# State-space stage of a four-layer forward pass: two of four tiles' sums by accumulating transfers, the dt projection in two halves, and one decay factor computed earlier on ScalarE

## The reference, cut to what matters

```python
xm, z = split(x @ W_in.T)                       # 512 channels each
xc = silu(causal_conv4(xm) + conv_b)
dt, Bm, Cm = split(xc @ W_xproj.T, [64, 64 + 16])
delta = softplus(dt @ W_dt.T + b_dt)
A = -exp(A_log)                                 # 512 x 16
h_t[:, n] = exp(delta_t * A[:, n]) * h_{t-1}[:, n] + delta_t * Bm_t[n] * xc_t     # n = 0..15
y_t = sum over n of Cm_t[n] * h_t[:, n] + D_skip * xc_t
out = (y * silu(z)) @ W_out.T
```

## Time and profile before

| | us |
|---|---|
| median of 3 runs | 2458.88 (2457.44 to 2459.68) |
| the profiled execution | 2460.9 |
| its span | 2459.2 |
| busy: PE / DVE / ACT / POOL over the span | 1911.8 / 1678.1 / 1184.7 / 1515.8 |
| the 8 halves of the loop, about | 68 to 1131 |

### The profile page before, as it was taken

How to read it: one execution, slowest core, us unless ns; L and a number is a source line. 1 busy time by engine, 2 the same in 40 slices (tenths; PEclk the granted TensorE clock), 3 DMA queues, 4 the chain that set the end, 5 groups by cost and what they waited for, 6 DMA issues and landing times. The chain is left out here.

```text
span 2459.2 us, 35798 instructions
## 1 busy us (share of the span) xinstructions
PE 1911.8 (78%) x10252; PEld 1465.2 (60%) x10253; DVE 1678.1 (68%) x3193; ACT 1184.7 (48%) x2021; POOL 1515.8 (62%) x1152
## 2 busy tenths in 40 slices
PE   6787879686979787875599999907877784799970
PEld 2445455554555454544499999904655664699970
DVE  1779898989989898985644444437634897644438
ACT  2677777777777767773232222226632441111112
POOL 1799999999999999994133333335622420355532
PEclk9888979798989888887699999958988896799995
DMA  3111111111101011112411111142000014122226
GB/s 123 38 35 40 39 37 36 39 39 37 39 23 52 27 49 31 43 36 77 165 48 47 47 48 48 41 139 77 9 18 11 9 35 163 42 71 70 70 65 192
DMA packets 76780, 138.63 MB, mean 56 GB/s; under 512 B 10369, under 2 KB 47873, under 8 KB 75858
## 3 DMA queue, kind: packets, MB, share of 16 engines
q1 hardware_dynamic: 62994, 99.67, 12.4%
q0 software_dynamic: 13632, 37.24, 4.8%
HBM read 104.86 MB, written 32.01 MB: 56 GB/s over the span
## 5 line engine op out<-in xcount | busy, mean ns | idle before, releaser
L787 DVE TENSOR_TENSOR_SCAN a_hs<-a_dA,a_carry,a_hs 128x512 f32<-128x512 f32 x512 | 628.3, 1264 | 63.5 <-ACT a_dA L559 53.7
L399 POOL TENSOR_TENSOR a_hs<-a_u,a_b_bc 128x1024 f32<-128x1024 f32 (+1 forms) x292 | 634.9, 2182 | 2.3 <-POOL a_u L381 1.9
L929 PE MATMUL a_h_ps<-k_ident,a_hs 128*128 128x128 f32 x2064 | 328.3, 308 | 174.7 <-DVE a_acc L750 95.6
L929 PEld LDWEIGHTS a_h_ps<-k_ident,a_hs 128*128 128x128 f32 x2064 | 268.4, 158 | 293.5 <-DVE a_hs L787 86.2
L559 ACT ACTIVATE a_dA<-a_delta,a_a_neg 128x512 f32<-128x512 f32 x512 | 350.1, 687 | 39.6 <-DVE a_hs L787 38.4
L411 POOL TENSOR_TENSOR a_acc<-a_acc,a_part 128x512 f32<-128x512 f32 x242 | 331.7, 1371 | 28.6 <-ACT a_part L573 28.3
L573 ACT ACTIVATE a_part<-a_h_ps,a_c_tok 128x512 f32<-128x512 f32 x242 | 166.0, 686 | 203.8 <-PE a_h_ps L929 176.0
L1229 POOL DMA_INDIRECT expert_rows<-m0e_ys,k_pair x71 | 78.7, 1109 | 232.5 <-DVE m0e_ys L1285 221.6
L750 DVE SCALAR_TENSOR_TENSOR a_acc<-a_h_ps,a_c_tok,a_acc 128x512 f32<-128x512 f32 x242 | 176.3, 728 | 46.5 <-PE a_h_ps L929 46.4
L863 PE MATMUL a_fx<-a_hT,a_w_x 128*128 128x512 f32 x432 | 200.9, 597 | 2.2 <-ACT a_halo L495 1.4
L1295 DVE TENSOR_TENSOR m0e_hT<-m0e_gs,m0e_u 128x512 f32<-128x512 f32 x70 | 48.2, 688 | 191.5 <-ACT m0e_gs L1248 191.5
(11 more groups left out here) (420 smaller groups left out, 3793.2 us busy)
## 6 DMA issues: line engine op xcount, KB each, us to landing
a_b_bc<-b_rows SPq DMA_DIRECT2D x132, 256.0 KB, 3.2
c_y<-expert_rows SPq DMA_DIRECT2D x16, 512.0 KB, 5.6
q_y<-expert_rows SPq DMA_DIRECT2D x16, 512.0 KB, 5.9
norm_rows<-a_x SPq DMA_DIRECT2D x9, 512.0 KB, 3.3
m0w_up<-in_m_up SPq DMA_DIRECT2D x1, 4096.0 KB, 12.1
m0w_gate<-in_m_gate SPq DMA_DIRECT2D x1, 4096.0 KB, 22.2
m0w_down<-in_m_down SPq DMA_DIRECT2D x1, 4096.0 KB, 32.1
c_xl<-in_L_attn_x SPq DMA_DIRECT2D x8, 512.0 KB, 3.7
```

Of the source, the lines that this page charges most:

```text
L399: last = pool.tensor_tensor(hs[k][:, w, :], u[s][:, w, :], b_bc[:, k:k + 1, :].broadcast_to([P, width, T]), ALU.mult)
L787: dve.tensor_tensor_scan(hs[k][:, c, :], dA[c][:], hs[k][:, c, :], carry[:, hf, c, n:n + 1], ALU.mult, ALU.add).then_inc(s_scan, 1)
L929: last = pe.transpose(hT_ps[j % 2][:, c * P:(c + 1) * P], hs[(n - 1) % NBUF][:, c, j * P:(j + 1) * P], ident[:])
```

## The change

- `add` on GpSimd becomes one transfer per step that accumulates both tiles of `part` into `acc` in SBUF (`accum_op=ALU.add`, 128 x 2 x 512 float32, 512 KB). It comes after both products, waits for the second weighted tile and for the transfer before it, and counts 16 on `s_add`. There are 15 per half.
- `part` is doubled: `weighted` writes copy n % 2 and waits for the transfer two before. The space comes from `hn`, which becomes another name for `x1`; so ScalarE's wait for the store of `x1` moves from step 14 to step 1.
- At the start GpSimd clears `part` too and runs two accumulating transfers of zeros, each waited for, before `front_power`.
- `dt` is cut into two parts of two matmuls: the first stays at the end of step 9, the second goes between the pairs of tiles of step 10.
- At the end of steps 8, 10 and 11 ScalarE computes the factor of chunk 3 before its tasks instead of after them.

```diff
-        hn = m.sb("hn", [P, TJ, D])
...
         x1 = m.sb("x1", [P, TJ, D])
+        hn = x1
...
-        part = m.sb("part", [P, TJ // 2, ED])
+        part = m.sb("part", [P, 2, TJ // 2, ED])
...
-                 11: ["d2", "d3"], 12: ["o0"], 13: ["z0"], 14: ["z3"], 15: ["r"]}
+                 10: ["dt.2", "dt.3"], 11: ["d2", "d3"], 12: ["o0"], 13: ["z0"], 14: ["z3"], 15: ["r"]}
...
-                7: ["xc2.3", "xc3.0"], 8: ["xc3.2", "xc3.3"], 9: ["dt"], 10: ["d0", "d1"], 11: ["ct"], 12: ["o1"], 13: ["z1", "z2"],
+                7: ["xc2.3", "xc3.0"], 8: ["xc3.2", "xc3.3"], 9: ["dt.0", "dt.1"], 10: ["d0", "d1"], 11: ["ct"], 12: ["o1"], 13: ["z1", "z2"],
...
+        LONG_END = (8, 10, 11)
...
-            pool.sem_inc(s_add, NO)
-            pool.wait_ge(s_const, 2)
+            pool.memset(part[:], 0.0).then_inc(s_const, 1)
+            pool.wait_ge(s_const, 4)
+            pool.sem_inc(s_prep, 1)
+            for k in range(2):
+                pool.dma_start(acc[1][:, OFF[0]:TJ:2, :], part[:, k], accum_op=ALU.add).then_inc(s_add, 16)
+                pool.wait_ge(s_add, 16 * (k + 1))
...
-            def add(U, n, j, s):
-
-                if j not in OFF or n == 1:
+            def add(U, n, s):
+
+                if n == 1:
                     return
-                pool.wait_ge(s_part, part_count(U, n, j))
-                if n == 0:
-                    pool.wait_ge(s_add, added_count(U, 0, j) + -NO)
-                elif n > 2:
-                    pool.wait_ge(s_add, added_count(U, n - 1, j))
-                pool.tensor_tensor(acc[s][:, j, :], acc[s][:, j, :], part[:, j // 2, :], ALU.add).then_inc(s_add, 1)
+                pool.wait_ge(s_part, part_count(U, n, OFF[-1]))
+                pool.wait_ge(s_add, added_count(U, n, 1))
+                pool.sem_inc(s_go, 1)
+                pool.dma_start(acc[s][:, OFF[0]:TJ:2, :], part[:, n % 2], accum_op=ALU.add).then_inc(s_add, 16)
...
                         for q in range(2):
                             product(U, ahead, q, hf if ahead < NS else 1 - hf)
-                            add(U, n, 2 * q + 1, hf if n else 1 - hf)
+                        add(U, n, hf if n else 1 - hf)
...
-                    act.wait_ge(s_add, added_count(U, 0, j) + -NO if n == 0 else added_count(U, n - 1, j))
-                    to = part[:, j // 2, :]
+                    if j == OFF[0]:
+                        act.wait_ge(s_add, added_count(U, n - 2) if n > 3 else added_count(U, 0, (2, None, 0, 1)[n]))
+                    to = part[:, n % 2, j // 2, :]
...
                         if n == 1:
+                            act.wait_ge(s_rst, lin(U, 16, 16))
                             act.wait_ge(s_pw, lin(F, 1, 1))
...
-                            act.wait_ge(s_rst, lin(U, 16, 16))
...
+                        if n in LONG_END:
+                            factor(U, n + 1, 3, there)
                         for name in END_ACT.get(n, []):
                             task(name)
-                        factor(U, n + 1, 3, there)
+                        if n not in LONG_END:
+                            factor(U, n + 1, 3, there)
...
-                    for c in range(EC):
+                    for c in range(EC) if part_ is None else (part_,):
```

More of the change, by code:

```diff
@@ L450, in _ @@
             end = (0, 2 * NB, None)
-            for j in OFF:
-                add(end, 0, j, 1)
+            add(end, 0, 1)
             rms(TILES - TJ, lambda per_: per_ * (2 * NB + 1))
@@ L954, in _ @@
             pe.wait_ge(s_acc, lin(end, NS * ND, 2 * ND))
-            pe.wait_ge(s_add, lin(end, ADDS, 2 * NO))
+            pe.wait_ge(s_add, added_count(end, 0))
             pe.wait_ge(s_da, 2 * NB * NS * EC + EC)
```

13 lines of the change are left out of this document (7 added, 6 removed).

## The result

| | before | changed |
|---|---|---|
| median, us | 2459.28 (4 runs) | 2497.48 (2495.96 to 2501.36, 4 runs) |
| span of the profiled execution | 2459.2 | 2496.8 |
| TensorE's first matmul | 17.25 | 32.98 |
| first `softplus_fix` of the loop to the last | 178.92 to 1087.33 | 192.40 to 1116.06 |
| mean distance of two fixes, us | 129.77 | 131.95 |

The ratio is 1.0156 [1.0139, 1.0174]: 38 us slower, where 28 us less was forecast. The time lies above the range.

A forecast was written before the change was run, and what follows sets the result against it. VectorE's work plus its waits was taken to bound each half, GpSimd close behind. Gains of 2.1 + 2.5 + 0.9 = 5.5 us per half, 44 in eight, less 9.6 and 6.2 at the ends, gave 2431 us; range 2395 to 2480.

The forecast's parts named there:

- What bounds the kernel: Whole half: VectorE's work plus 13.0 us of waits sets its length; taking 40.4 us off GpSimd gives nothing directly.
- Term 1: Steps 8 to 12: the moves on ScalarE and TensorE bring the fix forward by 2.1 us per half.
- Term 2: VectorE beside GpSimd: the add pair in step 13 runs free, 2.5 us per half; nothing taken for fix and sub.
- Term 3: Step 1: GpSimd reaches `front_power` some 3 us sooner, so waits for `nb` shrink, 0.9 us per half.
- Taken as nothing: `y0`, once per half: the last transfers land at 741.0 and 747.5 against its start at 747.34, so no cost.
- Term 4: An accumulating transfer's time, taken as 6.5 us, with its costs at start, end, `y0` and in the loop.
- The start: Prologue: a memset and two zero transfers in series make it start 9.6 us later (3.2 to 14.8).
- T: Time from a transfer's issue on GpSimd until `s_add` has counted it: 6.5 us, ends 3.3 and 9.1.
- The end: Behind the loop: the last two transfers must land before TensorE's output, 6.2 us later (1.6 to 11.4).
- Rival B: Fast steps: transfers become the clock, gain used up near 7 us each, about 2534 us at 8; chance 0.26.
- The sum: Whole program: 5.5 us less per half, 44 in eight, plus 9.6 and 6.2 at the ends: 2431 us.

The follow-up runs named there:

- run 1: The kernel before with only the moves on ScalarE and TensorE (dt in halves, chunk 3's factor first), adds still on GpSimd: 2457.18 us, ratio 0.9995.
- Runs 9: run 3's kernel with GpSimd holding the four shorts of step 12 until the fix pair is done: 2435.03 us, ratio 0.9889.
- run 5: run 3's kernel with a small zeroing on GpSimd and a wait for it behind each transfer's issue: 2463.54 us, ratio 1.0024.
- run 7: The kernel of run 1, with GpSimd waiting for its own adds in steps 11 and 12, no transfer: 2441.49 us, ratio 0.9930.
- Run 2: The changed kernel with the moves undone (dt whole, chunk 3's factor behind the long tasks), transfers kept: 2509.83 us, ratio 1.0203.
- run 4: The changed kernel with all accumulating transfers left out, the semaphore counted by GpSimd, sums left incomplete: 2427.53 us, ratio 0.9869.
- run 11: run 3's kernel with both edits: the four shorts held for the fix pair, and the last state's tiles summed by GpSimd adds: 2416.81 us, ratio 0.9817.
- runs 3: The changed kernel with the two zero transfers of the start put behind `front_power`: 2479.87 us, ratio 1.0092.
- run 10: run 3's kernel with the last state's two tiles summed by GpSimd adds, the other fourteen states by transfers: 2461.35 us, ratio 1.0001.
- run 13: The kernel before with only the hold: GpSimd waits in step 12 for the fix pair: 2464.99 us, ratio 1.0022.
- run 14: run 11's kernel with the hold extended from the fix pair to the sub pair and the zero transfers still later: 2468.98 us, ratio 1.0041.
- run 6: run 3's kernel with GpSimd waiting before every product for its product before it, shorts included: 2473.61 us, ratio 1.0058.
- run 15: run 11's kernel with a small zeroing and a wait for it behind each transfer's issue: 2430.52 us, ratio 0.9881.

## Why the prediction was wrong, step by step

- **What bounds the kernel: right.** VectorE's work plus its waits set the half. GpSimd's load fell by 23 us and gave nothing by itself.
- **Term 1, 2.1 us per half: right in kind, and near in size.** The rows are where they were put. From the start of `silus` to the fix it is 27.0 us in run 1 and 30.2 before, 3.2 less, of which 0.6 to 0.7 is the factor that now stands ahead of `silus`; so this stretch gave 2.5. The agreement of 127.4 with 127.7 for a whole half is partly luck: in those five halves the three VectorE pairs took 11.5 us together for 12.4 before, which is 0.9 of the 2.4 us.
- **Term 2 failed, and with it the forecast.** Its add pair was right: 2.35 us for 4.92, a gain of 2.57 where 2.5 was forecast. The step that failed is "For fix and sub I take nothing, as products should still lie beside them". The term gave these pairs a bound of a gain and none of a loss, though both moves and transfers change what stands beside them. The fix pair went from 3.51 to 5.98 or some 11 us, 41 us over the program; the sub pair did get shorter by 0.5 us a half. Runs 9 and 5 show that GpSimd's row beside the pair is the cause; run 7 shows it without transfers. Before, the row was broken by an add that waited 1.5 us for its tile, 2.3 us ahead of the pair; now four shorts follow an issue directly. Run 2 has the transfers without the moves, and its pair takes 6.59 us. That the moves add to it by bringing the fix earlier is likely, but not shown by itself.
- **Term 3, 0.9 us per half: wrong, small.** ScalarE's waits for `nb` came to 13.3 us in 6 times before and 13.9 in 6 after. GpSimd did not reach `front_power` sooner: ahead of it in the row stands the issue of the last state's transfer, which waited 2.1 to 3.7 us for the landing before it in five of the eight halves. Without transfers (run 4) ScalarE's wait is 2.6 us in one time.
- **`y0`, "Taken as nothing": wrong.** The estimate let the transfer land at 747.5 against a start at 747.34, with no margin for GpSimd's own order: the issue stands behind two products of the next state, and waits for both tiles. In the half around 240 us it was 16.9 us from the tile of state 15 to `y0`, not 13.0: 3.1 until the products ahead of the issue were done, 8.2 for that transfer, 0.6 to the next issue and 5.0 for the last one. TensorE's wait grew by 17 us; what it cost is less certain. The sum of the difference leaves 13 us for it and all else, and the traces of runs 9 and 11 show 8.9 us between the fixes, those of runs 3 and 10 only 1.6. The medians fell by 18 us in both pairs of runs, of which the end of the loop is 4 to 5.
- **Term 4, the time of a transfer:** 5.4 us in the loop for the 6.5 taken, right in size as a median, but not for the transfers that someone waited for (7.4 to 9.0 us ahead of `y0`). *The start* was undersized, 15.7 us for 9.6, because T was taken the same there, and the two zero transfers needed 18.9 us for 13 while the weights were loading. *The end* came out right, 6.3 us for 6.2, with T taken 1.1 us too long twice, so partly by luck. By the rule of the Trainium skill (DMA: Bandwidth & Descriptors, section Anatomy of one DMA) T would have been 3.2 us if an accumulation cost no more than a copy; the measured 5.4 decides against that.
- **Rival B did not happen,** though its sign was right. Its condition was T near 7; T was 5.4, and ScalarE never waited for a copy of `part` in the changed kernel. The loss came by another way than the one that had the chance of 0.26. A rival of this sort was missing: that the two-input instructions get slower, not faster. The row at 827.90 with 3.51 us for what takes 2.4 alone was the place to ask what decides between 2.4, 3.5 and more.
- **The sum.** With the fix held and the last state summed by adds (run 11) the fixes are 124.9 us apart, the forecast's 124. That is not the same sum: run 11 holds the fix pair at 2.36 us, 1.1 less than the forecast took, and lacks term 3. Most terms that were counted were good in size; the one that was waved through cost nearly as much as they were to bring.

## What to carry to other kernels

Where VectorE has instructions with two inputs in SBUF and GpSimd computes beside them, ask for each such place what GpSimd's row looks like, and whether there is a wait in it: work taken off GpSimd turned 3.5 us into 6.6 here (run 2), a step moved by 2 us turned it into 4.1 to 11 (run 1). A wait on purpose, for the VectorE instruction that must get in or for GpSimd's own last result, was cheap where GpSimd had idle time (run 9) and useless where it had little (run 13); look where the held work falls next (run 14 lost 52 us by it). A transfer that replaces an add brings throughput but a latency of several us (5.4 here): try the last link of each sum, the one that someone waits for, on an engine, and look what else then waits for the landing before it (run 10).

## What was not expected of the hardware

- A pair of two-input VectorE instructions (128x1024) took 2.36 us alone, 3.4 to 4.5 beside GpSimd instructions in a row recently broken by a wait, 5.98 or 6.59 beside four shorts behind an issue, and 8.2 to 11.8 beside longer rows in which GpSimd waited for nothing. In run 1 an add that had to wait for its tile 2.9 us before the pair, in one half without any idle time to be seen, went with 4.12 us in place of 8.2 to 10.95; four waits a half for own results (run 7) had the same effect.
- In the record a product begins 0.44 us before the transfer's issue ahead of it has ended (190.75 and 191.19), and each of the shorts behind it 0.5 us before the one ahead has ended; with a wait behind the issue (run 5) they no longer do. That GpSimd's parts are out of step fits this and the sentence of the Trainium skill quoted above (GPSIMD Engine Reference, Instruction dispatch); the records show no single part, so it is an inference, and for the long rows of run 1, whose records overlap by 0.03 to 0.07 us, they do not even hint at it.
- An accumulating transfer of 512 KB within SBUF landed in 5.4 us in the loop (median), with DMA engines 47% busy, in 7.4 to 9.0 us for that of state 15 in five halves, and in 9.0 to 9.5 us among the start's loads.
- Open: the waits before the wide products of run 6; what a wait changes inside GpSimd in rows without a transfer; how much of the time the landing at `y0` cost; and half of the loss of run 15.
